# A graph layer in fp32 on one core: attribute loads four groups ahead, clears with no limit in flight, gather ring of 11

## The reference, cut to what matters

```
h   = x @ W_in2f
Wij = (softplus(edge_attr @ Wf1 + bf1) - log 2) @ Wf2 + bf2     # 50,000 x 256
Wij = Wij * edge_weight
m   = segment_sum(h[dst] * Wij, src)                            # sums rows by their node
m   = (softplus(m @ Wo1 + bo1) - log 2) @ Wo2 + bo2
out = layernorm(x + (x + m))
```

## Time and profile before

| | us |
|---|---|
| median of 3 runs (lowest, highest) | 1875.04 (1873.83, 1876.91) |
| the profiled execution's own time | 1860.02 |
| its span, first to last instruction | 1858.3 |
| clearing, until the first scatter | 0 to 221.5 |
| scatters and gathers | 221.5 to 1400.1 |
| second phase | 1402.1 to 1858.3 |

### The profile page before, as it was taken

How to read it: one execution, slowest core, us unless ns; L and a number is a source line. 1 busy time by engine, 2 the same in 40 slices (tenths; PEclk the granted TensorE clock), 3 DMA queues, 4 the chain that set the end, 5 groups by cost and what they waited for, 6 DMA issues and landing times. The chain is left out here.

```text
span 1858.3 us, 36496 instructions
## 1 busy us (share of the span) xinstructions
PE 1747.4 (94%) x11376; PEld 1546.2 (83%) x11376; DVE 1506.0 (81%) x3750; ACT 1482.4 (80%) x2945; POOL 1428.4 (77%) x1385
## 2 busy tenths in 40 slices
PE   4689899999999999999999999989886999999995
PEld 3577788888888888888888888878776999999995
DVE  3567688888888888888888888876675999999996
ACT  3566688888887878787878787866666999999996
POOL 6542378878878878878878878778664999999997
PEclk9889999999999999999999999999997999999998
DMA  9999857666666666666666566677665899999994
GB/s 320 330 339 336 273 109 127 115 123 116 122 114 125 115 120 122 118 123 117 122 112 124 112 125 114 126 145 143 138 105 170 323 362 363 360 361 361 361 361 172
DMA packets 177339, 363.45 MB, mean 196 GB/s; under 512 B 25622, under 2 KB 76264, under 8 KB 177148
## 3 DMA queue, kind: packets, MB, share of 16 engines
q1 hardware_dynamic: 101128, 257.75, 40.7%
q0 software_dynamic: 75136, 102.45, 32.6%
q10 hardware_dynamic: 884, 0.92, 0.2%
HBM read 206.90 MB, written 154.12 MB: 194 GB/s over the span
## 5 line engine op out<-in xcount | busy, mean ns | idle before, releaser
L358 POOL DMA_INDIRECT acc<-sums,src_ix x392 | 633.2, 1615 | 171.4 <-issue 120.9
L344 POOL DMA_INDIRECT xg<-in_x,dst_t x392 | 392.2, 1000 | 200.7 <-issue 107.6
L389 POOL TENSOR_SCALAR sums<-sums,neg_mean,rstd 128x256 f32<-128x256 f32 x392 | 283.4, 735 | 10.2
L625 ACT ACTIVATE m_h<-pair,wgt_t 128x256 fp32r<-128x256 f32 x392 | 164.2, 475 | 113.3 <-PE pair L413 113.3
L499 PE MATMUL pair<-m_h,same 128*128 128x256 f32 (+1 forms) x980 | 248.0, 288 | 1.2 <-DVE m_l L786 1.2
L499 PE MATMUL pair<-m_l,same 128*128 128x256 f32 (+1 forms) x980 | 242.2, 282 | 0.0
L413 PE MATMUL pair<-wo_h,msg_h 128*128 128x256 f32 (+1 forms) x784 | 234.5, 299 | 4.0 <-DVE m_l L786 1.9
L769 DVE SCALAR_TENSOR_TENSOR pair<-pair,bias_w,h_sb 128x512 f32<-128x512 f32 x196 | 147.8, 754 | 108.2 <-PE pair L413 108.1
L413 PE MATMUL pair<-wo_l,msg_h 128*128 128x256 f32 (+1 forms) x784 | 223.1, 285 | 0.0
L413 PE MATMUL pair<-wo_h,msg_l 128*128 128x256 f32 (+1 forms) x784 | 222.1, 283 | 0.0
L531 PE MATMUL pair<-w_in_h,ssp_l 128*128 128x256 f32 (+1 forms) x784 | 220.2, 281 | 0.0
(11 more groups left out here) (96 smaller groups left out, 5394.3 us busy)
## 6 DMA issues: line engine op xcount, KB each, us to landing
acc<-fill SPq DMA_DIRECT2D x197, 256.0 KB, 3.8
xg<-in_x SPq DMA_DIRECT2D x97, 512.0 KB, 6.1
sums<-acc SPq DMA_DIRECT2D x97, 512.0 KB, 6.7
out<-sums SPq DMA_DIRECT2D x97, 512.0 KB, 4.7
attr<-in_edge_attr SPq DMA_DIRECT2D x196, 128.0 KB
srcb<-in_src_rows SPq DMA_DIRECT2D x98, 256.0 KB
xg<-in_x,dst_t POOLq DMA_INDIRECT x392, 3.7
acc<-sums,src_ix POOLq DMA_INDIRECT x392
```

The source lines that it names most:

```text
L344: pool.indirect_dma_start(xg[0:g.p, g.xs, r], None, t["x"], bass.IndirectOffsetOnAxis(ap=dst_t[0:g.p, r, g.n:g.n + 1], axis=0)).then_inc(x ...
L358: pool.indirect_dma_start(acc, bass.IndirectOffsetOnAxis(ap=src_ix[g.slot][0:g.p, r:r + 1], axis=0), sums[0:g.p, g.slot, r], None, compute ...
L389: last = pool.tensor_scalar(normed[0:g.p, g.n % NRING, r], res[0:g.p, u, r], neg_mean[0:g.p, u, r:r + 1], rstd[0:g.p, u, r:r + 1], ALU.add ...
L625: act.activation(m_h[0:g.p, r], bank[6][0:g.p, k * D:(k + 1) * D], ACT.Copy, scale=col(wgt_t, r, g)).then_inc(mh_sb, 1)
```

## The change

Four edits:

- `ARING` goes from 2 to 4. SP loads attributes 0 to 3 before the first clear, and in pass n of its loop those of group n+4, which wait for `a_low` of group n.
- The loop is counted from n = 0 and pass n loads `src` rows of group n (the same wait as before: comparisons of group n-2). 36 clears are issued first and 15 in each pass (was 16).
- The clears share one semaphore and don't wait for one another (`IN_FLIGHT` is gone). Pool waits for all of them at one value.
- `XRING` goes from 12 to 11 and `AHEAD` from 24 to 23. So 92 gathers come before the first scatter and 300 behind it (was 96 and 296). In the second phase 11 groups of `x` instead of 12 are loaded before it, and the twelfth inside it.

```diff
-XRING = 12
-ARING = 2
+XRING = 11
+ARING = 4
-AHEAD = 24
+AHEAD = 23
-IN_FLIGHT = 4
-CLEARS_A_STEP = 16
+CLEARS_A_STEP = 15
...
-        cleared = [sem(f"cleared{u}") for u in range(IN_FLIGHT)]
+        cleared = sem("cleared")
...
-            load_attr(1)
+            for n in range(1, ARING):
+                load_attr(n)
...
-                    wait(sp, cleared[c % IN_FLIGHT], c // IN_FLIGHT * 16)
                     sp.dma_start(acc[a:b, :].rearrange("(p k) d -> p (k d)", k=CLEAR),
-                                 fill[0:(b - a) // CLEAR].rearrange("p k d -> p (k d)")).then_inc(cleared[c % IN_FLIGHT], 16)
+                                 fill[0:(b - a) // CLEAR].rearrange("p k d -> p (k d)")).then_inc(cleared, 16)
...
-            for n in range(2, G + 1):
-                if n < G:
-                    load_attr(n)
-                load_src(n - 1)
-                clear_to(FIRST_CLEARS + (n - 1) * CLEARS_A_STEP)
-                if G - XRING <= n - 2:
-                    fetch_x(group((n - 2) % XRING))
+            for n in range(G):
+                if n + ARING < G:
+                    load_attr(n + ARING)
+                if n:
+                    load_src(n)
+                clear_to(FIRST_CLEARS + (n + 1) * CLEARS_A_STEP)
+                if G - XRING <= n:
+                    fetch_x(group(n % XRING))
...
-            for n in range(G - 1, G):
-                fetch_x(group(n % XRING))
...
-                            for u in range(IN_FLIGHT):
-                                pool.wait_ge(cleared[u], 16 * len(range(u, CLEARS, IN_FLIGHT)))
+                            pool.wait_ge(cleared, 16 * CLEARS)
```

## The result

| | before | changed |
|---|---|---|
| median, us (lowest, highest; runs) | 1875.45 (1873.83, 1876.91; 4) | 1845.95 (1843.59, 1850.03; 4) |
| ratio of the runs, 95% interval | 1 | 0.9845 [0.9823, 0.9867] |
| profiled execution's own time | 1860.02 | 1843.96 |
| its span | 1858.3 | 1842.2 |
| first scatter | 221.51 | 194.68 |

The two profiled executions differ by only 16.1 us, since that of before was itself 15 us quicker than the kernel's other runs. By their spans: 26.8 us won until the first scatter, 8.2 lost from there to the transposes of group 97 (1139.4 us before, 1147.6 after), 1.2 in the tail behind them and 1.3 in the second phase (456.2 us, then 457.5).

A forecast was written before the change was run, and what follows sets the result against it. Bound: DMA work until the clears end, then Pool's work up to the last gather, then a tail. Terms -5.5 + 5.1 - 12 = -12.4 us, carried to the median: 1875 - 12 = 1863 us, range 1850 to 1878.

The forecast's parts named there:

- Term 1: Clearing stage, when the clears end: better filling, fewer gathers and load order give -5.5 us; ends -1.6 and -14.
- Filling: Clearing stage: clears queued without a limit raise the DMA share to 0.98 throughout, -3.9 us.
- Full rate: Rival, clearing stage: deep queues bring 359 GB/s, -14 us there; 1854, or 1847 with all of Term 3; chance 0.14.
- Slower: gathers stand behind the clears: Rival, clearing stage: gathers wait for a backlog of about 20 clears, +66 us, about 1929; chance 0.06.
- Term 2: Pool after the clears: four more gathers behind them, 1.285 us each, +5.1 us on the path.
- Term 3: Pool's waits before scatter 0: one 512 KB load burst becomes two of 256 KB, -12 us; ends nothing and 18.8.
- all 18.8: Far end of Term 3: all 18.8 us of Pool's waits above the fixed gap before scatters are saved.
- Term 4: Beside the other terms: TensorE may be 28 us earlier by its own work; stock, tail and second phase cost 0.
- the things that would show the prediction wrong: First scatter hardly moving, gathers landing far later, scatter 0 waits staying at 18 us, or src_ix waits long before group 92.
- the other signs: Expected: first scatter about 216 us, share 0.98, 300 gathers behind, issue waits about 0.33 us, attributes 5 us before rows.
- the sum: Whole span: -5.5 + 5.1 - 12 = -12.4 us on 1858.3, so 1845.9.

The follow-up runs named there:

- e4: Kernel before with only the waits between clears taken out (no limit on clears in flight): 1834.94 us, ratio 0.985 to before.
- e7: Changed kernel with at most eight clears in flight: 1833.87 us, ratio 0.9821 to before.
- e2: Changed kernel with at most four clears in flight again: 1839.04 us, ratio 0.9881 to before.
- e1: Kernel before, unchanged, profiled again: 1862.07 us (before on that chip 1861.67).
- e11: Changed kernel with at most four clears in flight, on the same chip as e9: 1854.02 us, ratio 0.9941 to before.
- e9: Kernel before, unchanged, on a third chip: 1865.05 us (before on that chip 1865.34).
- e6: Changed kernel with 24 groups gathered before the first scatter instead of 23, in the same 11 slots: 1831.05 us, ratio 0.9807 to before.
- e5: Changed kernel, unchanged, profiled again: 1834.42 us (before on that chip 1866.64), ratio 0.9839.
- e8: Changed kernel with XRING 12, ARING 3 and 24 groups gathered ahead: 1830.35 us, ratio 0.9802 to before.
- e17: Kernel of e8 (rings of 12 and 3, 24 ahead, loads apart) run again: 1832.04 us (before on that chip 1867.08), ratio 0.9803.
- e18: Kernel of e17 with the two loads of a pass in one burst: 1835.58 us, ratio 0.9829 to before.
- e10: Changed kernel, unchanged, on the same chip as e9: 1831.98 us, ratio 0.9819 to before.
- e12: Changed kernel with rows then attributes loaded in one burst, on the same chip as e9: 1831.77 us, ratio 0.9829 to before.
- e13: Changed kernel, unchanged (no limit, loads apart), on a fourth chip: 1847.31 us (before on that chip 1870.93), ratio 0.9861.
- e14: Changed kernel with the two loads in one burst, no limit, on the same chip as e13: 1840.34 us, ratio 0.9834 to before.
- e15: Changed kernel with at most four clears in flight, loads apart, on the same chip as e13: 1872.72 us, ratio 1.0005 to before.
- e16: Changed kernel with at most four clears in flight and loads in one burst, on the same chip as e13: 1867.66 us, ratio 0.9983 to before.
- the first set: Four runs on one chip, e1, e2 and e4 among them, each compared with before there; before took 1861.67 us.
- the third: Third set: e9, e10, e11 and e12 on one chip, each compared with before there; before took 1865.34 us.
- the fourth: Fourth set: e13 to e16, limit or none by loads apart or together, on one chip; before took 1870.93 us.

## Why the prediction was wrong, step by step

**The step that failed is Term 1, its part "Filling".** It read the DMA share of 0.96 as 96% of what the engines can do, took 0.98 as full because the second phase shows it, and took the second phase's 359 GB/s as the far end. Hence -3.9 us, -5.5 with the rest, and -14 at most. Measured: 384 GB/s at a share of 1.05 and a first scatter 26.8 us earlier (26.7 in e4, where nothing else changes). The sentence "so the stage ends when the DMA engines have done their work" was the error behind it: e7 and e2 show that the stage ended when clears came back, four at a time. The sizes of the small parts don't matter beside this; e2, which has all of Term 1 but the filling, came 5.2 us earlier than e1, where -1.6 was counted for that, with single records to compare (e11 against e9 has 3.3).

The rival "Full rate" had the mechanism, deep queues, and was sized by the same false ceiling. Beside it stood the Trainium skill's 358 GB/s ("DMA: Bandwidth & Descriptors", Specifications). The Trainium skill also says ("HBM Reference", Specifications (TRN2)) that 358 is a core's share when both cores of a pair stream, and that a core alone measures about 425 GB/s. This kernel runs on one core, and its 379 to 389 GB/s without a limit lie between the two figures: they agree with that sentence, not with the line that the prediction drew on.

**"Slower: gathers stand behind the clears" didn't happen.** Pool's waits from 8 to 195 us in the changed kernel:

```profile
POOL xg L342 <- DMA xg<-in_x,dst_t: 74.2, 34, 4.9
```

Pool's waits for landings grew from 33.9 us (26 times) to 74.2 (34 times), but the longest is 4.9 us, where a landing of 13 us would have decided. The 92 gathers were out at 185.4 us, before the clears ended. But the rival's condition, some 20 clears queued, is not seen either. The prediction has 51 clears "issued at once"; SP took 0.72 us for each of the first 36 and ended the last twelve 4 us before the first scatter:

```profile
8.78 26.01 SPq L272 DMA_DIRECT2D acc<-fill  x36
...
181.87 8.85 SPq L272 DMA_DIRECT2D acc<-fill  x12
```

In the 26 us of the first row the DMA, at 383 GB/s, moves as much as 38 clears, so few can have piled up. In the last 4 us no more than six can pass, so no more were waiting then. In e6, where SP was done 9.8 us before, it can have been 15 at most, and its longest such wait over the whole stage is 4.4 us. What a backlog of 20 would do these runs don't show.

**Term 2, +5.1 us**, is borne out in part: gathering the four ahead again gave -3.4 (e6, its interval touches e5's) and, with the rings, -4.1 us (e8). The profiled executions don't show it all: the transposes of group 97 start at 1328.87 in e5, 1331.35 in e6 and 1328.72 in e8.

**Term 3, -12 us**, had the right mechanism for the waits. In every set the kernels with the loads apart have 0.3 to 2.8 us of excess waits before groups 1 to 50 and those with them together 5.0 to 11.4. Its size depends on something that the prediction didn't know. Where steps take 13.17 us it is more than forecast: between the first scatter and the last gather e1 has 24.9 us of waits over the gaps and e2 5.8. That is -19, the end "all 18.8" rather than -12; with +3.8 us for four more gathers and their gaps and -2.9 for shorter scatters it makes the 17.8 us above, within 0.4. Where steps take 13.4 us or more the medians of the four pairs say 3.5 us won (e17, e18), nothing (e10, e12), 7.0 lost (e13, e14) and 5.1 lost (e15, e16). None of the four is clear of its intervals. In three of them the waits for `src_ix` grow where the others shrink; in e17 and e18, up to group 88, there are none.

**Term 4, "what lies beside", failed second.** It said that TensorE can only be earlier and has 28 us in hand. That counted with 13.17 us a step, by which the transposes of group 97 could have started at 182.68 + 85 x 13.17 = 1302 us. They started at 1342.23, and gathers are not the reason: from 1100 to 1345 us TensorE waits for them only 1.6 us:

```profile
PE pair L421 <- DMA xg<-in_x,dst_t: 1.6, 2, 1.1
```

So of the 26.8 us of the clears 17.4 arrive at the start of the second phase in the recorded pair. Between the first scatter and the transposes of group 97 Terms 2 and 3 forecast 6.9 us less, and the record has 8.2 us more. The sign for it stood among the things that would show the prediction wrong: the scatters wait for `src_ix` long before group 92, from 72 on.

**Of the other signs** 300 gathers stand behind the first scatter, the loads go out 5 to 6 us apart, Pool's "issue" waits before a scatter average 52.8 / 171 = 0.31 us, and tail and second phase are as before within 1.3 us each. TensorE's first wait for a gather behind the first scatter was to come well before 1219 us and came at 1330. The first scatter (216 forecast, 194.7) and the share (0.98, 1.05) are the two that went with Term 1. The errors partly cancel: Term 1 was 21 us too weak in size, Term 3 too strong for the runs that were timed. That the span of 1842.2 us is near the 1845.9 of the sum is luck of this kind. The medians fell by 29.5 us and the two profiled executions by 16.1, because the step from 1860 to 1875 us, which the prediction carried over from the kernel before, is not in the changed kernel's runs (1843.96 profiled, 1845.95 median); why the kernel before took 15 us more in its other runs stays open.

## What to carry to other kernels

A DMA share near 1.00 does not prove that the DMA is full when the issuing engine waits for its own transfers. Divide the bytes in flight by the rate that you hope for (four clears at 384 GB/s: 2.7 us); if that is less than the time that one transfer is under way (some 4 us here), the limit holds the rate down. Try twice the number in flight before anything else. A ceiling read in another stage of the kernel is that stage's rate, not the chip's. And where two engines are close in pace (Pool 11.9 us a group and TensorE 13.17 a step here), work out how much one must slow down before it sets the end, and keep that in the range.

## What the hardware showed that was not expected

**A core alone moved more than the second phase suggested.** 69.83 MB in 182 us, of which q1 57.04 and the gathers' software queue 12.06, in the changed kernel from 8 to 190 us (packets, MB, share of 16 engines):

```profile
q1 hardware_dynamic: 31564, 57.04, 85.0%
q0 software_dynamic: 4416, 12.06, 18.3%
```

**TensorE's signals came late in most recordings.** In the records of before, e1 and e2, none of the 662 to 667 semaphore updates of TensorE's matmuls between 200 and 1000 us comes over 0.5 us after the end of the matmul that gives it. In those of the changed kernel 107 of 511 do, 172 us in all, and 128 further ones are missing from the record; in e5 it is 81, in e10 70, in e13 113. In the changed kernel's timeline the product that `m_h` reads ends at 253.4 us by the record (its last matmul starts at 253.16), and ScalarE starts only at 255.71, with a releaser that the profile can't name:

```profile
253.16 0.28 PE L410 MATMUL pair<-wo_h,msg_l 128*128 128x256 f32 x1
...
255.71 0.84 ACT L622 ACTIVATE m_h<-pair,wgt_t 128x256 fp32r<-128x256 f32 x2 [3.23 <-remote]
...
256.66 0.48 DVE L783 SCALAR_TENSOR_TENSOR m_l<-pair,wgt_t,m_h 128x256 fp32r<-128x256 f32 x1 [2.48 <-ACT m_h L622]
```

Where that happens, steps take 13.4 to 14.0 us (in the changed kernel's record at the same granted clock of 1.00, with waits of TensorE for `m_l` and `msg_l`). The more of it, the longer the steps: the lateness adds up to 95 to 115 us in the ten recordings with steps of 13.39 to 13.58 us, and to 168 to 180 us in the five with 13.74 to 14.03. It goes with the set and the chip, not with the edit: before has it in e9 and not in e1. The longer steps are in the timed runs too: one and the same kernel with the limit of four and the loads apart has a ratio of 0.9881 in the first set, 0.9941 in the third and 1.0005 in the fourth, in the order of their steps (13.18, 13.39, 14.03). Whether the late signals are the cause of the longer steps, or both come from something else, stays open. So does what makes a chip or a set do it, and what the changed kernel would take without it.
